# Attention tail of a convolution-and-attention network on one core: final projection by image against final projection by unit

## The chip, the cores and the metric

The kernel runs on one core of a Trainium2 chip. The metric is the device time of one execution in microseconds, the median of three runs.

## What is computed

The input is 8 images of 56x56 positions with 128 channels, all in fp32. A first block (group norm, gated long convolution by FFT, residual) gives `x`. The second block, where the change lies, normalizes `x` by groups, mixes heads within every position and adds the result to `x`:

```python
q, k, v = xs @ Wq.T, xs @ Wk.T, 2 * (xs @ Wv.T)        # 8 heads of 16
q, k, v_h = _l2norm(q), _l2norm(k), _l2norm(v)
attn_head = softmax(einsum('bnhd,bngd->bnhg', v_h, v_h))
q = einsum('bnhg,bngd->bnhd', attn_head, q)
k = einsum('bnhg,bngd->bnhd', attn_head, k)
attn = softmax(einsum('bnhd,bnhe->bnde', k, q))
out = einsum('bnhd,bnde->bnhe', v, attn)
out = transpose(out, (0, 3, 1, 2)).reshape(b, n, HEADS * DIM_HEAD)
out = out @ proj_w.T + proj_b
x = x + out
```

The transpose before the last projection matters here. It runs over (batch, e, position, head) and the result is read again as rows of 128: output row e x 196 + r of an image (e is one of 16 numbers of a head, r one of 196) gathers e of all 8 heads of 16 neighbouring positions. So the output row e x 196 + r needs the attention of positions 16 r to 16 r + 15 alone.

## The kernel before

The program is written by hand: each engine has its list of instructions, and semaphores (`wait_ge`, `then_inc`) order them. Stages follow each other: weights, first normalization and projection, taps, convolution (the longest), its output, and `attend` (from line 989), which starts at about 2214.8 us of the span. Only `attend` and one constant's load are touched.

`attend` cuts the 25088 positions into 56 blocks of 448 (4 tiles of 112), and each block into 2 **units** of 224 positions: 14 groups (`GU`) of 16 positions, with (position, head) on the 128 partitions. There are 112 units (`NU`), 14 per image (`UPI`), and round i of the main loop works at several of them. On PE a round is, in this order:

- `scores(i+1)`: 28 matmuls into `ps_s` (two banks); ScalarE exponentiates (`exp_s`), VectorE masks (`mask`),
- `outputs(i-2)`: 28 matmuls into `ps_o`; VectorE moves them to `oT` (`leave`),
- `mix(i)`: 28 matmuls into `ps_mix`; ScalarE (`leave_mix`) and VectorE (`weigh`) take them, GpSimd spreads k to blocks,
- `logits(i-1)`: 56 matmuls into `ps_l`; ScalarE exponentiates (`exp_l`), VectorE normalizes (`divide`: z_sum, z_inv, p_norm),
- in some rounds a **final group**, `final(b, u)`,
- two `project` calls, the q, k, v projections of tiles 8 rounds ahead, into `ps_qkv` and `ps_qkv_fin` in turn; ScalarE squares and copies them (`copy_in`), VectorE sums and normalizes (`squares`, `clamp`, `normalize`), and ScalarE writes them to memory (`store_heads`), from where SyncE's queue loads them with another layout (`turn`). In every second round ScalarE takes a square root (`root`), for which it loads another table and then the exp table again.

The last projection needs, for a row, one e and the 8 heads of 16 positions, and that is a column of `oT`: 128 (position, head) partitions of group r. The kernel before collects `oT` for a whole image (128 x 16 x 196), and in eight final groups (u = 0 to 7) makes the image's rows: four values of e by 98 of r, each a matmul with `oT`'s 98 columns as the weights and the 128x128 matrix moving, plus a second matmul that adds the residual `x1` through the identity, into the same bank. The bank is `ps_qkv_fin`, the one of the odd projection. VectorE adds the bias, broadcast over partitions (`res`), ScalarE's queue stores. `FINS` sets the rounds: (b + 1) x 14 + 3 + u. So rounds 17 to 24, 31 to 38 and so on have a final group, the six after them none, and the last image's eight groups come behind all units, in rounds 115 to 122. In rounds with a final group, PE waits between its two projections:

```python
if i in FINS:
    b, u = FINS[i]
    pe.wait_ge(f_r, b * 8 + u + 1)
project(bk + 1)
```

Projections end with round 103. The residual `x1` has one buffer, loaded again after an image's last group. In the profile `x_in` of this stage is `x1`, since numbers of buffers are left out of names.

Of the kernel before, what the change touches and what calls it, by code (L numbers as in the profile page):

```python
# [70 lines left out]
def load_weights(nc, t, k):  # L71


    with ExitStack() as ctx:
# [29 lines left out]
                     (k.proj_b[:], t.L1_conv_proj_b.rearrange("(a o) -> a o", a=1).to_broadcast([128, CH]))]  # L104
# [884 lines left out]
def attend(nc, t, k):  # L989
# [12 lines left out]
    RH = RPI // 2  # L1002
    with ExitStack() as ctx:
# [28 lines left out]
        ps_a, ps_m, ps_o, ps_f = (psum(n) for n in ("ps_qkv", "ps_mix", "ps_o", "ps_qkv_fin"))  # L1032
# [4 lines left out]
        x1_loaded = sem("x1_loaded")  # L1037
        out_stored = [sem(f"out_stored{m}") for m in range(4)]
# [5 lines left out]
        o_ps, o_r, f_ps, f_r = (sem(n) for n in ("o_ps", "o_ready", "fin_ps", "fin_ready"))  # L1044
        block = ctx.enter_context(nc.Block())
        FINS = {}
        for b in range(BATCH):
            for u in range(8):
                FINS[(b + 1) * UPI + 3 + u] = (b, u)
        ROUNDS = (BATCH) * UPI + 3 + 8  # L1050
# [46 lines left out]
        def _(pe):  # L1097
# [12 lines left out]
            def scores(i):  # L1110
# [3 lines left out]
                if i:  # L1114
                    pe.wait_ge(s_exp, i)
                v = vb[n % NIN]
# [40 lines left out]
            def final(b, u):  # L1157
                lo, e0 = u // 4 * RH, u % 4 * 4
                if u == 0:
                    pe.wait_ge(o_r, (b + 1) * UPI)  # L1160
                    pe.wait_ge(x1_loaded, 16 * (b + 1))
                if b * 8 + u:
                    pe.wait_ge(f_r, b * 8 + u)
                pe.wait_ge(qkv_read, min(NB * BPB, AHEAD * BPB + 2 * (b * UPI + UPI + 3 + u)))
# [10 lines left out]
            for i in range(ROUNDS):  # L1175
# [9 lines left out]
                if i in FINS:  # L1185
                    final(*FINS[i])
                if bk < NB * BPB:
                    project(bk)
                    if i in FINS:
                        b, u = FINS[i]  # L1190
                        pe.wait_ge(f_r, b * 8 + u + 1)
                    project(bk + 1)

        @block.scalar
        def _(act):
# [43 lines left out]
            def store(b, u):  # L1239
                act.wait_ge(f_r, b * 8 + u + 1)  # L1240
                lo, e0 = u // 4 * RH, u % 4 * 4
                rows = t.out_rows[b * TOK:(b + 1) * TOK].rearrange("(e r) c -> r e c", e=HD)
                act.dma_start(rows[lo:lo + RH, e0:e0 + 4, :], res[u % 4][:]).then_inc(out_stored[u % 4], 16)
                if u == 7 and b + 1 < BATCH:
                    act.dma_start(x1[:], t.X1[b + 1]).then_inc(x1_loaded, 16)

            act.dma_start(x1[:], t.X1[0]).then_inc(x1_loaded, 16)
# [8 lines left out]
            for i in range(ROUNDS + 1):  # L1256
# [9 lines left out]
                if unit(i - 1):  # L1266
                    exp_l(i - 1)
                if bk < NB * BPB:
                    copy_in(bk)
                    copy_in(bk + 1)  # L1270
                if i in FINS:
                    store(*FINS[i])
            for m in range(4):
                act.wait_ge(out_stored[m], 16 * 2 * BATCH)
# [190 lines left out]
```

## Time and profile before

| | |
|---|---|
| median of 3 runs | 3543.01 us (3539.26 to 3554.57) |
| the profiled execution's own time | 3533.34 us |
| its span, first to last instruction | 3531.5 us |
| mean granted TensorE clock | 0.951 |
| PE busy | 3160.9 us, 90% of the span |
| VectorE, ScalarE, GpSimd busy | 2083.4, 1486.9, 251.6 us |
| `attend` in the span | 2214.8 to 3531.5 us |

PE's busy time is made of pipelined matmuls, whose records overlap, and covers time in which it isn't at its peak. What is worth reading is when one group of matmuls starts and the next: the distance of starts, and what PE waited for where there is a gap. A matmul in fp32 has two records (x56 for 28), a transpose one.

### The profile page before, as it was taken

How to read it: one execution, taken by the hardware profiler on the slowest of the kernel's cores; microseconds unless marked ns; L12 is line 12 of the kernel's file. 1: busy time of each engine (PE TensorE's matmuls, PEld its weight loads, DVE VectorE, ACT ScalarE, POOL GpSimd, SP SyncE). 2: the span in 40 equal slices, each digit the busy share in tenths (PEclk: the TensorE clock that was granted, in tenths of full speed). 3: DMA queues.
4: the chain of work that ended last, by engine and by line, in shares of the span. 5: the costliest groups of instructions: out<-in, count | busy, mean ns of one | idle time of the engine just before them, and what ended most of it. 6: DMA issues, size and time to landing. Idle time of an engine off the chain costs nothing. (4 is left out here: it accounts for less than half of the span.)

```text
span 3531.5 us, 106371 instructions
## 1 busy us (share of the span) xinstructions
PE 3160.9 (90%) x44223; PEld 2406.7 (68%) x44223; DVE 2083.4 (59%) x3840; ACT 1486.9 (42%) x3254; POOL 251.6 (7%) x162
## 2 busy tenths in 40 slices
PE   5686977999999999999999898589898989898887
PEld 4563324777777777777777544477777877777777
DVE  4453553666666666666666577455555555555553
ACT  3454422444444444444444344454444444444431
POOL 0000000000000000000000022211111111111111
PEclk8787978999999999999999999799999999999999
DMA  6886004111211211111112497655555555555552
GB/s 149 252 215 177 1 0 160 49 48 48 49 48 48 49 49 48 48 49 49 48 49 49 165 404 311 130 82 87 107 88 106 93 98 88 104 104 87 106 83 52
DMA packets 1033978, 351.36 MB, mean 99 GB/s; under 512 B 888569, under 2 KB 1005991, under 8 KB 1028519
## 3 DMA queue, kind: packets, MB, share of 16 engines
q1 hardware_dynamic: 710832, 198.81, 25.7%
q10 hardware_dynamic: 322807, 147.46, 15.3%
q8 instruction: 282, 4.62, 0.5%
q14 instruction: 57, 0.47, 0.0%
HBM read 174.01 MB, written 172.15 MB: 98 GB/s over the span
## 5 line engine op out<-in xcount | busy, mean ns | idle before, releaser
L751 ACT ACTIVATE x_half<-ps_x 56x228 f32<-56x228 f32 x1024 | 366.1, 357 | 671.8 <-PE ps_x L693 662.9
L801 DVE TENSOR_TENSOR terms<-spec,ps_z 112x456 f32<-112x456 f32 x1024 | 573.0, 621 | 33.8 <-PE ps_z L701 28.7
L708 PEld LDWEIGHTS ps_q<-inv_w,prod 112*114 112x114 f32 x4096 | 434.9, 180 | 27.5 <-issue 25.5
L708 PE MATMUL ps_q<-inv_w,prod 112*114 112x112 f32 x4096 | 451.0, 263 | 0.9 <-DVE prod L805 0.9
L701 PE MATMUL ps_z<-x_half,fwd_w 120*112 120x456 f32 x1024 | 446.4, 558 | 0.9
L811 DVE COPY y_sb<-ps_y 112x224 f32<-112x224 f32 x256 | 100.1, 391 | 414.2 <-PE ps_y L716 331.7
L1143 PE MATMUL ps_l<-q_mixed,k_blocks 32*64 32x64 f32 x12544 | 231.8, 220 | 74.1 <-issue 73.4
L1094 POOL TENSOR_TENSOR k_blocks<-k_mixed,same_of 128x896 f32<-128x896 f32 x112 | 193.8, 1730 | 1072.4 <-ACT k_mixed L1237 1072.4
L1143 PEld LDWEIGHTS ps_l<-q_mixed,k_blocks 32*64 32x64 f32 x12544 | 206.1, 133 | 88.5 <-issue 79.8
L1120 PEld LDWEIGHTS ps_s<-v_blocks 128*64 128x64 f32 x6272 | 200.9, 141 | 90.5 <-issue 79.2
L693 PEld LDWEIGHTS ps_x<-fwd_h,v_in 96*120 96x120 f32 x2048 | 256.2, 185 | 8.0 <-issue 3.2
L693 PE MATMUL ps_x<-fwd_h,v_in 96*120 96x114 f32 x2048 | 256.2, 268 | 1.7 <-ACT x_half L751 1.7
L716 PEld LDWEIGHTS ps_y<-q_half,inv_h 114*112 114x112 f32 x1024 | 179.2, 176 | 114.8 <-issue 95.2
L701 PEld LDWEIGHTS ps_z<-x_half,fwd_w 120*112 120x112 f32 x1024 | 160.7, 176 | 124.9 <-issue 111.6
L1120 PE MATMUL ps_s<-v_blocks 128*64 128x64 f32 x6272 | 218.9, 228 | 23.2 <-issue 14.7
L716 PE MATMUL ps_y<-q_half,inv_h 114*112 114x224 f32 x1024 | 236.4, 352 | 1.3 <-ACT q_half L778 1.3
L1132 PE MATMUL ps_mix<-qk_rows,e_blocks 64*64 64x64 f32 x6272 | 212.9, 220 | 10.0 <-issue 9.8
L1154 PE MATMUL ps_o<-p_norm,v_blocks 128*64 128x64 f32 x6272 | 208.6, 224 | 11.3 <-DVE p_norm L1327 8.0
L1305 DVE TENSOR_TENSOR e_blocks<-s_exp,same_of 128x896 f32<-128x896 f32 x112 | 121.9, 1088 | 153.6 <-ACT s_exp L1222 153.6
L1132 PEld LDWEIGHTS ps_mix<-qk_rows,e_blocks 64*64 64x64 f32 x6272 | 195.1, 135 | 20.2 <-issue 12.3
L1154 PEld LDWEIGHTS ps_o<-p_norm,v_blocks 128*64 128x64 f32 x6272 | 198.0, 140 | 12.6 <-DVE p_norm L1327 8.1
L1281 DVE TENSOR_REDUCE nsq<-sq 112x48 f32<-112x768 f32 x112 | 106.7, 953 | 161.4 <-ACT qkv L1206 161.4
(128 smaller groups left out, 4488.7 us busy)
## 6 DMA issues: line engine op xcount, KB each, us to landing
conv_in<-v_sb ACTq DMA_DIRECT2D x112, 256.0 KB, 3.3
v_in<-conv_in SPq DMA_DIRECT2D x256, 112.0 KB
qk_heads<-st_qk ACTq DMA_DIRECT2D x56, 476.0 KB, 4.7
qk_rows<-qk_heads SPq DMA_DIRECT2D x56, 476.0 KB, 6.7
conv_out<-y_sb ACTq DMA_DIRECT2D x512, 49.0 KB
y<-conv_out SPq DMA_DIRECT2D x8, 1792.0 KB, 13.5
x_in<-in_x SPq DMA_DIRECT2D x8, 1568.0 KB, 9.7
shortcut<-short ACTq DMA_DIRECT2D x8, 1568.0 KB, 6.3
```

The lines of the kernel that those rows point to most:

```text
L693: last = pe.matmul(ps_x[0:120, c * 2 * NF:(c + 1) * 2 * NF], v_in[b % 2][:, c * 2 * PADW:c * 2 * PADW + 120], k.fwd_h[:], start=True, stop ...
L701: last = pe.matmul(ps_z[b % 2][x][0:NFFT, 0:PC], k.fwd_w[:, x, :], x_half[b % 2][:].rearrange("p c a f -> p (c a f)"), start=True, stop=True)
L708: last = pe.matmul(ps_q[0:2 * NF, c * NFFT:(c + 1) * NFFT], prod[b % 2][:, x, c * 2 * NF:(c + 1) * 2 * NF], k.inv_w[:, x, :], start=(x == ...
L716: last = pe.matmul(ps_y[0:2 * SIDE, 0:CC // 2 * SIDE], k.inv_h[:, x, :], q_half[:, :, x, :], start=(x == 0), stop=(x == 1))
L751: last = act.activation(x_half[b % 2][to:to + SIDE, :, a], src, ACT.Copy)
L801: last = dve.tensor_tensor(terms[:, x, :], spec[a][:, s, :], ps_z[b % 2][z][0:NFFT, 0:PC], ALU.mult)
L1094: pool.tensor_tensor(kb[i % 2][:], bcast(km[i % 2][:], 3, 4), bcast(bcast(k.same4[:], 1, HD), 1, GU), ALU.mult).then_inc(k_r, 1)
L1120: last = pe.matmul(to, v[:, gb, a, :], v[:, gb, a, :], start=True, stop=True)
L1132: last = pe.matmul(ps_m[rows, g * QKM:g * QKM + 64], eb[i % 2][rows, g, :], strided(qk[n % NIN][rows], gb * QKW, [[1, 64]]), start=True, s ...
L1143: last = pe.matmul(ps_l[half:half + 64, s // 2, g * HD:g * HD + 64], kb[i % 2][rows, g].rearrange("p d m -> p (d m)"), qm[i % 2][rows, g:g ...
L1154: last = pe.matmul(ps_o[64 * a:64 * a + 64, g * HD:g * HD + 64], vb[n % NIN][:, gb, a, :], pn[i % 2][:, a, g:g + 4, :], start=True, stop=True)
L1305: dve.tensor_tensor(eb[i % 2][:], ex[i % 2][:], bcast(k.same8[:], 1, GU), ALU.mult).then_inc(e_r, 1)
```

## The change

The final projection is made per unit, with the output channels on the partitions:

- `final(i)` is one matmul: the 128x128 matrix as the weights, `oT` of the unit (now 128 x 16 x 14, two buffers) as 224 moving columns, into the first bank of `ps_s`, where the scores of unit i + 3 have just been read. It stands in round i + 2, behind the logits.
- VectorE adds bias (now one number per partition) and residual in one scalar_tensor_tensor (`add`) and writes `y_fin`.
- `turn_out(i)`, in round i + 3, transposes `y_fin` in two halves of 112 columns into `ps_o`; ScalarE copies them (`copy_out`), and its queue stores them in two transfers.
- `x1` has two buffers, and those of the first two images are loaded at the start.
- `FINS` and the eight rounds behind the last unit are gone (`ROUNDS` is `NU + 4`), as is PE's wait between projections. `ps_qkv_even` and `ps_qkv_odd` are new names of the projections' banks.
- New waits: `scores(i)` for `add(i-4)`, `outputs(i)` for `copy_out(i-2)` in place of `leave(i-1)`, `turn_out(i)` for `add(i)` and `leave(i+1)`.

```diff
@@ attend @@
-        oT = [sb(f"oT{m}", [128, HD, RPI]) for m in range(2)]
-        x1 = sb("x1_in", [128, TOK])
-        res = [sb(f"res{m}", [RH, 4, CH]) for m in range(4)]
+        oT, y1 = ([sb(f"{n}{m}", [128, HD, GU]) for m in range(2)] for n in ("oT", "y_fin"))
+        x1 = [sb(f"x1_in{m}", [128, HD, RPI]) for m in range(2)]
+        res = [sb(f"res{m}", [TB, 2, CH]) for m in range(3)]
...
-        ROUNDS = (BATCH) * UPI + 3 + 8
+        ROUNDS = NU + 4
@@ PE: scores @@
                 if i:
                     pe.wait_ge(s_exp, i)
+                if i >= 4:
+                    pe.wait_ge(f_r, i - 3)
@@ PE: outputs @@
                 pe.wait_ge(p_r, i + 1)
-                if i:
-                    pe.wait_ge(o_r, i)
+                if i >= 2:
+                    pe.wait_ge(t_r, i - 1)
@@ PE @@
-            def final(b, u):
-                lo, e0 = u // 4 * RH, u % 4 * 4
...
-                for e in range(4):
-                    to = ps_f[0:RH, e * CH:(e + 1) * CH]
-                    pe.matmul(to, oT[b % 2][:, e0 + e, lo:lo + RH], k.w[:, PW, :], start=True, stop=False)
-                    at = (e0 + e) * RPI + lo
-                    last = pe.matmul(to, x1[:, at:at + RH], k.ident[:], start=False, stop=True)
-                last.then_inc(f_ps, 1)
+            def turn_out(i):
+                pe.wait_ge(f_r, i + 1)
+                pe.wait_ge(o_r, min(i + 2, NU))
+                if i:
+                    pe.wait_ge(t_r, i)
+                for h in range(2):
+                    last = pe.transpose(ps_o[0:TB, h * CH:(h + 1) * CH], y1[i % 2][:, 8 * h:8 * h + 8, :].rearrange("p e g -> p (e g)"), k.ident[:])
+                last.then_inc(t_ps, 1)
+
+            def final(i):
+                pe.wait_ge(o_r, i + 1)
+                pe.wait_ge(s_exp, min(i + 4, NU))
+                pe.matmul(ps_s[:, 0, 0:HD * GU], k.w[:, PW, :], oT[i % 2][:].rearrange("p e g -> p (e g)"), start=True, stop=True).then_inc(f_ps, 1)
@@ PE: the round, behind logits(i - 1) @@
-                if i in FINS:
-                    final(*FINS[i])
+                if unit(i - 3):
+                    turn_out(i - 3)
+                if unit(i - 2):
+                    final(i - 2)
                 if bk < NB * BPB:
                     project(bk)
-                    if i in FINS:
-                        b, u = FINS[i]
-                        pe.wait_ge(f_r, b * 8 + u + 1)
                     project(bk + 1)
@@ ScalarE @@
+            def copy_out(i):
+                m = i % 3
+                act.wait_ge(t_ps, i + 1)
...
+                act.activation(res[m][:].rearrange("p h c -> p (h c)"), ps_o[0:TB, 0:2 * CH], ACT.Copy).then_inc(t_r, 1)
+
+            def store(i):
+                m, b, r0 = i % 3, i // UPI, i % UPI * GU
+                act.wait_ge(t_r, i + 1)
+                rows = t.out_rows[b * TOK:(b + 1) * TOK].rearrange("(h e r) c -> h e r c", h=2, e=8)
+                for h in range(2):
+                    act.dma_start(rows[h, :, r0:r0 + GU, :], res[m][:, h, :]).then_inc(out_stored[m], 16)
...
@@ VectorE @@
             def leave(i):
...
+            def add(i):
                 b, r0 = i // UPI, i % UPI * GU
+                dve.wait_ge(f_ps, i + 1)
...
+                if i >= 2:
+                    dve.wait_ge(t_ps, i - 1)
+                dve.scalar_tensor_tensor(out=y1[i % 2][:], in0=ps_s[:, 0, 0:HD * GU].rearrange("p (e g) -> p e g", g=GU), scalar=k.proj_b[:, 0:1],
+                                         in1=x1[b % 2][:, :, r0:r0 + GU], op0=ALU.add, op1=ALU.add).then_inc(f_r, 1)
@@ VectorE: the round, behind divide(i - 1) @@
-                if i in FINS:
-                    add_bias(*FINS[i])
+                if unit(i - 2):
+                    add(i - 2)
```

How the order moves on PE. Before, a round with a final group, from its logits to the next round's outputs (`x27` counts matmuls of one form):

```order
L1143 MATMUL ps_l<-q_mixed,k_blocks 64x64 [waits l_exp_ready,k_blocks_ready,q_mixed_ready]
L1143 MATMUL ps_l<-q_mixed,k_blocks 64x64 x55
L1167 MATMUL ps_qkv_fin<-weights,oT 98x128 [waits qkv_read,fin_ready]
L1169 MATMUL ps_qkv_fin<-ident,x_in 98x128
...
L1104 MATMUL ps_qkv<-weights,xn_in 112x384 [waits qkv_read,xn_loaded0]
L1104 MATMUL ps_qkv_fin<-weights,xn_in 112x384 [waits qkv_read,fin_ready]
L1120 MATMUL ps_s<-v_blocks 64x64 [waits s_exp_ready,in_loaded2]
L1120 MATMUL ps_s<-v_blocks 64x64 x27
L1154 MATMUL ps_o<-p_norm,v_blocks 64x64 [waits o_ready,p_ready]
```

Changed, the same place, in every round:

```order
L1140 MATMUL ps_l<-q_mixed,k_blocks 64x64 [waits l_exp_ready,k_blocks_ready,q_mixed_ready]
L1140 MATMUL ps_l<-q_mixed,k_blocks 64x64 x55
L1160 MATMUL ps_o<-ident,y_fin 112x128 [waits turned_ready,o_ready,fin_ready]
L1160 MATMUL ps_o<-ident,y_fin 112x128
L1166 MATMUL ps_s<-oT,weights 128x224 [waits s_exp_ready,o_ready]
L1099 MATMUL ps_qkv_even<-weights,xn_in 112x384 [waits qkv_read]
L1099 MATMUL ps_qkv_odd<-weights,xn_in 112x384 [waits qkv_read]
L1117 MATMUL ps_s<-v_blocks 64x64 [waits fin_ready,s_exp_ready]
L1117 MATMUL ps_s<-v_blocks 64x64 x27
L1151 MATMUL ps_o<-p_norm,v_blocks 64x64 [waits turned_ready,p_ready]
```

The wait for `fin_ready` has moved from the odd projection in some rounds to the scores in all of them. On VectorE, changed, where it is set:

```order
L1331 TENSOR_REDUCE z_sum<-p_exp 128x28 [waits l_exp_ready]
L1333 RECIPROCAL z_inv<-z_sum 128x28 [waits z_ready]
L1337 TENSOR_TENSOR p_norm<-p_exp,z_inv 128x2x224 [waits o_ps,z_inv_ready]
L1354 SCALAR_TENSOR_TENSOR y_fin<-ps_s,proj_b,x_in 128x224 [waits turned_ps,fin_ps]
L1291 TENSOR_REDUCE nsq<-sq 112x48 [waits qkv_read]
```

`y_fin`, which sets `fin_ready`, stands where `res` (98x512, line 1343) stood in rounds with a final group, now in every round.

## Rows read from the trace of the kernel before

**Rows 1.** Windows: busy us of each engine (x instructions), PEclk, DMA share, GB/s.
```profile
2275.60:3468.20 1192.60, 1062.55 (x31266) 912.20 (x31265) 664.27 (x1221) 546.69 (x1201) 185.41 (x107) 0.98 0.55 94
...
2589.00:2683.00 94.00, 85.77 (x2407) 73.72 (x2408) 53.19 (x98) 42.59 (x95) 13.68 (x8) 1.00 0.56 93
```

**Rows 2.** Timeline, PE, scores opening rounds 2, 17, 25, 31, 39, 109.
```profile
2275.60 0.62 PE L1120 MATMUL ps_s<-v_blocks 128*64 128x64 f32 x13
...
2432.21 0.50 PE L1120 MATMUL ps_s<-v_blocks 128*64 128x64 f32 x9
...
2527.08 0.51 PE L1120 MATMUL ps_s<-v_blocks 128*64 128x64 f32 x10
...
2588.97 0.51 PE L1120 MATMUL ps_s<-v_blocks 128*64 128x64 f32 x10
...
2682.82 0.50 PE L1120 MATMUL ps_s<-v_blocks 128*64 128x64 f32 x9
...
3468.20 0.62 PE L1120 MATMUL ps_s<-v_blocks 128*64 128x64 f32 x13
```

**Rows 3.** Timeline, PE, round 72, without a final group.
```profile
3053.49 1.85 PE L1120 MATMUL ps_s<-v_blocks 128*64 128x64 f32 x56
...
3060.47 0.90 PE L1104 MATMUL ps_qkv<-weights,xn_in 128*112 128x384 f32 x2
...
3061.94 0.28 PE L1120 MATMUL ps_s<-v_blocks 128*64 128x64 f32 x2
```

**Rows 4.** Timeline, PE, round 77, with one.
```profile
3122.01 0.46 PE L1167 MATMUL ps_qkv_fin<-weights,oT 128*98 128x128 f32 x2
...
3125.02 0.90 PE L1104 MATMUL ps_qkv_fin<-weights,xn_in 128*112 128x384 f32 x2 [0.37 <-DVE res L1343]
3125.84 0.34 PE L1120 MATMUL ps_s<-v_blocks 128*64 128x64 f32 x4
```

**Rows 5.** Waits of PE, rounds 2 to 109: total us, times, longest us.
```profile
PE ps_l L1143 <- issue: 73.4, 57, 3.1
```

**Rows 6.** Timeline, PE, transposes of the first stage.
```profile
252.48 0.55 PE L285 MATMUL ps_turn<-ident,x_in 112*128 112x112 f32 x4
252.86 0.86 PE L290 MATMUL ps_sumsq<-ones,x_sq 128*112 128x1 f32 x8
```

**Rows 7.** Timeline, VectorE, round 77.
```profile
3122.72 0.62 DVE L1321 TENSOR_REDUCE z_sum<-p_exp 128x28 f32<-128x448 f32 x1 [1.08 <-ACT p_exp L1228]
...
3123.74 0.62 DVE L1327 TENSOR_TENSOR p_norm<-p_exp,z_inv 128x448 f32<-128x448 f32 x1
3124.28 0.68 DVE L1343 TENSOR_TENSOR res<-ps_qkv_fin,proj_b 98x512 f32<-98x512 f32 x1
```

**Rows 8.** Timeline, ScalarE, then VectorE, round 72.
```profile
3054.81 1.28 ACT L1210 ACT_TABLE_LOAD   x1
...
3060.31 0.39 DVE L1316 TENSOR_TENSOR q_mixed<-ps_mix,d_sq_inv 128x224 f32<-128x224 f32 x1
3061.18 0.62 DVE L1321 TENSOR_REDUCE z_sum<-p_exp 128x28 f32<-128x448 f32 x1 [0.48 <-ACT p_exp L1228]
```

**Rows 9.** Groups, VectorE: busy us, mean ns | idle before, releaser.
```profile
L1335 DVE TENSOR_TENSOR oT<-ps_o,qk_rows 128x224 f32<-128x224 f32 x112 | 62.3, 556 | 10.3 <-PE ps_o L1154 10.3
...
L1316 DVE TENSOR_TENSOR q_mixed<-ps_mix,d_sq_inv 128x224 f32<-128x224 f32 x112 | 43.8, 391 | 5.3 <-DVE d_sq_inv L1311 0.2
...
L383 DVE SCALAR_TENSOR_TENSOR short<-xT,biases,xg 128x448 f32<-128x448 f32 x56 | 37.6, 672 | 0.5
```

**Rows 10.** Timeline, PE and the ACT queue, at the end.
```profile
3506.57 0.46 PE L1167 MATMUL ps_qkv_fin<-weights,oT 128*98 128x128 f32 x2 [0.65 <-DVE oT L1335]
...
3528.73 0.33 ACTq L1243 DMA_DIRECT2D out<-res  x1
```

**Rows 11.** Groups, ScalarE; then DMA issues (KB, us to landing).
```profile
L1204 ACT ACTIVATE sq<-ps_qkv 112x256 f32<-112x256 f32 x112 | 43.0, 384 | 161.9 <-PE ps_qkv L1104 155.2 <-issue 3.3 <-DVE st_v L1298 3.3
...
x_in<-x_mid ACTq DMA_DIRECT2D x8, 1568.0 KB, 7.9
```

More of the change, by code:

```diff
@@ L1028, in attend @@
         pn = [sb(f"p_norm{m}", [128, 2, GU + 3, HD]) for m in range(2)]
-        oT = [sb(f"oT{m}", [128, HD, RPI]) for m in range(2)]
-        x1 = sb("x1_in", [128, TOK])
-        res = [sb(f"res{m}", [RH, 4, CH]) for m in range(4)]
-        ps_a, ps_m, ps_o, ps_f = (psum(n) for n in ("ps_qkv", "ps_mix", "ps_o", "ps_qkv_fin"))
+        oT, y1 = ([sb(f"{n}{m}", [128, HD, GU]) for m in range(2)] for n in ("oT", "y_fin"))
+        x1 = [sb(f"x1_in{m}", [128, HD, RPI]) for m in range(2)]
+        res = [sb(f"res{m}", [TB, 2, CH]) for m in range(3)]
+        ps_a, ps_m, ps_o, ps_f = (psum(n) for n in ("ps_qkv_even", "ps_mix", "ps_o", "ps_qkv_odd"))
         ps_s, ps_l = psum("ps_s", (128, 2, 512)), psum("ps_l", (128, 2, 512))
@@ L1036, in attend @@
         in_loaded = [sem(f"in_loaded{m}") for m in range(NIN)]
-        x1_loaded = sem("x1_loaded")
-        out_stored = [sem(f"out_stored{m}") for m in range(4)]
+        x1_loaded = [sem(f"x1_loaded{m}") for m in range(2)]
+        out_stored = [sem(f"out_stored{m}") for m in range(3)]
         cleared, k_r, qkv_ps, qkv_read = sem("cleared"), sem("k_blocks_ready"), sem("qkv_ps"), sem("qkv_read")
@@ L1043, in attend @@
         l_ps, l_exp, z_r, zi_r, p_r = (sem(n) for n in ("l_ps", "l_exp_ready", "z_ready", "z_inv_ready", "p_ready"))
-        o_ps, o_r, f_ps, f_r = (sem(n) for n in ("o_ps", "o_ready", "fin_ps", "fin_ready"))
+        o_ps, o_r, f_ps, f_r, t_ps, t_r = (sem(n) for n in ("o_ps", "o_ready", "fin_ps", "fin_ready", "turned_ps", "turned_ready"))
         block = ctx.enter_context(nc.Block())
[L1046 to L1049, printed above, removed]
-        ROUNDS = (BATCH) * UPI + 3 + 8
+        ROUNDS = NU + 4
         def unit(i):
@@ L1237, in leave_mix, with load_x1 @@
                 act.activation(km[i % 2][:], ps[:, :, HD + 1:], ACT.Copy).then_inc(km_r, 1)
[L1239 to L1247, printed above, removed]
+            def load_x1(b):
+                act.dma_start(x1[b % 2][:].rearrange("p e r -> p (e r)"), t.X1[b]).then_inc(x1_loaded[b % 2], 16)
+            def copy_out(i):
+                m = i % 3
+                act.wait_ge(t_ps, i + 1)
+                if i >= 3:
+                    act.wait_ge(out_stored[m], 32 * (i // 3))
+                act.activation(res[m][:].rearrange("p h c -> p (h c)"), ps_o[0:TB, 0:2 * CH], ACT.Copy).then_inc(t_r, 1)
[5 more added lines that the diff above has]
+                    act.dma_start(rows[h, :, r0:r0 + GU, :], res[m][:, h, :]).then_inc(out_stored[m], 16)
+                if i % UPI == UPI - 1 and b + 2 < BATCH:
+                    act.wait_ge(f_r, (b + 1) * UPI)
+                    load_x1(b + 2)
+            for b in range(2):
+                load_x1(b)
             for bk in range(AHEAD * BPB):
@@ L1267, in _ @@
                     exp_l(i - 1)
+                if unit(i - 3):
+                    copy_out(i - 3)
                 if bk < NB * BPB:
@@ L1270, in _ @@
                     copy_in(bk + 1)
-                if i in FINS:
-                    store(*FINS[i])
-            for m in range(4):
-                act.wait_ge(out_stored[m], 16 * 2 * BATCH)
+                if unit(i - 3):
+                    store(i - 3)
+            for m in range(3):
+                act.wait_ge(out_stored[m], 32 * ((NU - 1 - m) // 3 + 1))
         @block.vector
@@ L1387, in build @@
         k.rpe_in = sb("rpe_in", [3, 128])
-        k.proj_b = sb("proj_b", [128, CH])
+        k.proj_b = sb("proj_b", [128, 1])
         k.same4, k.same8 = sb("same_of_4", [128, 4]), sb("same_of_8", [128, 64])
```

30 lines of the change are left out of this document (9 added, 21 removed).

## The prediction

> **What bounds the kernel now.** I read the page first (the diff touches the last stage alone), then the timeline of that stage by engine, then its waits. Scores of one round to scores of the next make a round. Between the scores of round 2 and those of round 109 lie 1192.60 us, 107 rounds of 11.15 us, in which PE is busy 1062.55 us at a mean clock of 0.98 [rows 1, 2]. So PE is what ends a round; the other engines follow it. Of the 107 rounds, 56 carry a final group (8 for each of seven images, rounds 17 to 24, 31 to 38 and so on) and 51 do not.
>
> A round without a disturbance shows the clean price. Scores at 3053.49, the first projection at 3060.47, the next scores at 3061.94: 6.98 us from scores to the end of the logits, and a **gap** of 1.47 us for the two projections, 8.45 us in all [rows 3]. With a final group the gap is 3122.01 to 3125.84, 3.83 us: the finals, the projections, and 0.37 us in which the second of these waits for VectorE's `res` [rows 4]. Such a round is 6.98 + 3.83 = 10.81 us clean.
>
> Real rounds are longer. Two groups of 8 final rounds, 2432.21 to 2527.08 and 2588.97 to 2682.82, take 188.72 us, 11.80 each; the 6 rounds between them take 61.89 us, 10.32 each [rows 2]. The **rest** over clean is 0.99 us with a final group and 1.87 us without. Most of it is PE idle with "issue" as releaser, 73.4 us ahead of the logits alone, in 57 stalls [rows 5]. The same instructions stall less where the gap is longer.
>
> **What the change takes away.** The eight matmuls of a final group, their wait, the wait of the odd projection for `res`, and the burst after the last unit. With it goes VectorE's `res` (0.68 us, 64 times).
>
> **What it puts into each round's gap, on PE.** Two transposes: four of 112 columns follow each other in 252.86 - 252.48 = 0.38 us, 0.10 each [rows 6]; at 128 columns 0.11 each, 0.22. One projection with 224 moving columns: the ones with 384 columns stand 0.74 us apart (half of 1.47), so 0.43. PE alone would need 0.22 + 0.43 + 1.47 = 2.12 us for the gap.
>
> **What it puts behind the logits, on VectorE.** `scores(i+2)` now waits for `f_r`, which is `add(i-2)`, since the final projection borrows `ps_s`. In VectorE's order `add` stands behind `divide`, and `divide` needs the logits just ended. From the end of the logits (3122.01) z_sum starts 0.71 us later, p_norm at 3123.74, and the next VectorE operation at 3124.28, 2.27 us after the logits [rows 7]. That chain has the same length in a round without a final group (z_sum at 3061.18, 0.71 after 3060.47 [rows 3, 8]). Then comes `add`, an operation the trace does not have in this shape. From below: a tensor_tensor from PSUM on 128x224 takes 0.391 us. From above: `res` with 512 elements, 0.68. A scalar_tensor_tensor on 448 elements takes 0.672 against 0.62 of p_norm, a tensor_tensor on as many, so the second operation with its scalar costs 0.05 [rows 7, 9]. I take 0.391 + 0.05 = 0.44, nearest to the operation with the same 224 elements, and 0.05 us to PE, as from `res` to the projection behind it (3124.28 + 0.68 = 3124.96, 3125.02) [rows 4, 7]. The gap is 2.27 + 0.44 + 0.05 = **2.76 us**, 0.64 more than PE needs: a new wait of PE ahead of the scores in every round. Clean round: 6.98 + 2.76 = 9.74.
>
> **The rest over clean.** Bounds 0.99 and 1.87. The new gap is 1.29 us longer than the short one, of the 2.36 between short and long, which in proportion gives 1.39; a disturbance of up to 0.64 us that falls in the gap disappears in the wait, so I take 1.30. A round is 11.04, 107 of them 1181.3, against 1192.6: **-11.3 us**.
> The Trainium skill (Runtime: NRT & Kernel Launch, section Instruction fetch mechanics) has instructions refilled in 16 KiB blocks at a cost it calls mostly hidden. Here it isn't hidden, if the "issue" stalls are these refills. By that rule the rest would be 0 on both sides: now 51 x 8.45 + 56 x 10.81, less 5 x 1.84 for the last five final rounds, which have no projections, 1027; changed 107 x 9.74 = 1042; +15 in place of -11.
>
> **The end.** Now the first final matmul of the last eight groups starts at 3506.57, the last store is issued at 3528.73 and the span ends at 3531.5, 2.8 later [rows 10]. Changed: one projection of 224 columns from 3506.57 until about 3507.2 (0.43 and the pipe's latency), `add` 0.44 to 3507.7, two transposes to 3508.1, one copy of 112x256 at 0.384 [rows 11] to 3508.6, then the same 2.8 for the store: 3511.5, **-20**. Round 109 and what follows it has a longer gap, +1.
>
> **The beginning.** Two images of the residual are loaded at once instead of one; one takes 7.9 us to land [rows 11] and it lies ahead of the first stores of heads on the same queue, which come some 20 us after. Between 0 and 8, I take +2.
>
> **Costed at nothing.** The bias column load, one of many loads; `leave` writing a smaller tile. ACT's copy (0.384) follows the logits' exp while PE still transposes and projects, and outputs two steps on need it only 1.7 us into the next round. Two stores per unit are issued at 0.33 each [rows 10] on ACT's queue, ahead of the square root's table load of every other round, behind which stand s_exp, the mask, `leave`, and so `turn_out` and z_sum. Now that load starts at 3054.81, 1.32 us after the scores, and VectorE ends q_mixed at 3060.70, 0.48 before z_sum [rows 8]. With the change ACT's copies of qkv end 0.65 later, the scores start 1.29 later, and the stores add 0.66: 0.02 later against the scores. If the cover of 0.48 goes, each us more costs a us in every other round.
>
> Sum: -11.3 - 20 + 1 + 2 = **-28 us**. The profiled execution took 3533.34 us (span 3531.5); it becomes 3505. It stands 9.7 below the median of 3543.0, so a median of **3515** is predicted.
>
> **The rivals.**
> 1. *The stalls shrink as far as in rounds with a final group.* Even spread helps every refill. Rest 0.99: 107 x 10.73 = 1148.1, -44.5, with the ends -61.5: 3482. For it: the whole drop came with a gap that held PE for 2.36 us longer, and the first part of it may do most. Against: only 0.64 is pure waiting.
> 2. *`add` is as dear as `res`,* by strided reading or PSUM access: 0.68 gives a gap of 3.00, +26: 3541. For it: `oT`, which also has strided operands, takes 0.556 with 224 elements [rows 9].
> 3. *The other side: the stalls stay as in rounds without a final group.* They sit mostly ahead of the logits [rows 5], and that stretch has its 6.98 us of the same instructions whatever the gap. Rest 1.87: 107 x 11.61 = 1242.3, +49.7, with the ends +33: 3576. It turns the sum positive from a rest of 1.56, and past 0.5% from 1.73. Against it: final rounds, with the same instructions there, have 0.99.
> 4. *The clock falls.* With idle time in every gap the granted clock could drop more often than its 0.98 [rows 1]. At 0.94, a half-clock share of 12% in place of 4%, 8% of 9.1 us of work in 107 rounds adds 78: 3593. The final groups, which wait 0.37 in each round, ran at 1.00 between 2589 and 2683, which speaks against it [rows 1]. The Trainium skill (TensorE: Matmul & The Clock Gate, A second HAM failure mode: psum-queue depth-cycling) describes this swing for a kernel that idles briefly between groups.
> 5. *The burst at the end isn't shortened,* since the chain through five engines is slower than counted: 3535.
>
> **How the numbers follow.** Forecast 0.45, rival 1 0.18, rival 2 0.20, rival 3 0.11, rival 4 0.04, rival 5 0.02. A measurement of this kernel can tell about 0.5% (17.7 us) from no change: faster means below 3525.3. Of the forecast 0.37 lies there and 0.08 within; with rival 1 faster is 0.55; rivals 2 and 5 and that 0.08 make 0.30 the same; 3 and 4 make 0.15 slower. The range, 3480 to 3565, reaches to half of rivals 1 and 3 and leaves out 0.19.
>
> **What would show it.** PE idle ahead of `ps_s` with `y_fin` as releaser, 0.6 us in nearly each of 104 rounds or more; a gap of 2.7 to 2.8 in clean rounds; `y_fin` at 0.44; "issue" idle ahead of the logits of 50 to 70 us between the scores of rounds 2 and 109, now 73.4 [rows 5]; the last scores to the end 20 shorter. I am wrong if PE does not wait for `y_fin` (the chain was not last), if 6.98 has grown (outputs or `turn_out` waiting), or if the clock is under 0.96.

## The result, and the profile after

| | before | changed |
|---|---|---|
| median, range | 3543.91 us (3539.26 to 3554.57, 4 runs) | 3590.56 us (3584.89 to 3596.18, 4 runs) |
| profiled execution, span | 3533.34, 3531.5 us | 3586.99, 3585.1 us |
| scores of round 2 to scores of round 109 | 1192.60 us | 1251.57 us |

The changed kernel takes 1.0128 times as long (95% interval 1.0112 to 1.0144). 3515 was predicted, with 3565 as the upper end; it is slower by more than the 0.5% that can be told from no change.

Windows of the changed kernel, columns as in [rows 1]:

```profile
2290.74:3542.31 1251.57, 1035.63 (x30796) 893.31 (x30795) 672.79 (x1271) 571.81 (x1305) 181.90 (x107) 0.96 0.53 90
```

PE is busy 27 us less than before and the stretch is 59.0 us longer, at a mean clock of 0.96 after 0.98 [rows 1]. The profiled executions differ by 53.7 us. These 59.0 are the main part. The tail behind the scores of round 109 is 42.8 us after 63.3, -20.5; from `attend`'s start to round 2 it is 63.4 after 60.8, +2.6; the stages ahead of `attend`, which the change doesn't touch, end 12.5 us later. That last part is scatter: a second profile of the kernel before, below, reaches round 2 at 2289.17, the first at 2275.60 [rows 2].

A round without a disturbance, changed kernel, timeline of PE and then of VectorE; it answers to [rows 3, 4, 7]:

```profile
3072.01 1.85 PE L1117 MATMUL ps_s<-v_blocks 128*64 128x64 f32 x56 [0.74 <-DVE y_fin L1354]
...
3078.99 0.43 PE L1160 MATMUL ps_o<-ident,y_fin 128*112 128x128 f32 x2
3079.26 0.54 PE L1166 MATMUL ps_s<-oT,weights 128*128 128x224 f32 x2
3079.64 0.81 PE L1099 MATMUL ps_qkv_even<-weights,xn_in 128*112 128x384 f32 x2
3080.29 0.81 PE L1099 MATMUL ps_qkv_odd<-weights,xn_in 128*112 128x384 f32 x2
3081.86 0.36 PE L1117 MATMUL ps_s<-v_blocks 128*64 128x64 f32 x5 [0.76 <-DVE y_fin L1354]
```

```profile
3079.71 0.62 DVE L1331 TENSOR_REDUCE z_sum<-p_exp 128x28 f32<-128x448 f32 x1 [1.48 <-ACT p_exp L1223]
...
3080.72 0.62 DVE L1337 TENSOR_TENSOR p_norm<-p_exp,z_inv 128x448 f32<-128x448 f32 x1
3081.27 0.44 DVE L1354 SCALAR_TENSOR_TENSOR y_fin<-ps_s,proj_b,x_in 128x224 f32<-128x224 f32 x1
```

From the scores to the end of the logits it is 6.98 us, as before. The new wait of PE for `y_fin` is there, and the gap is 3081.86 - 3078.99 = 2.87 us. The clean round is 9.85.

Waits of PE between the scores of rounds 2 and 109: total us, times, longest us. The releaser "issue" means that PE waited for nothing that the profile shows. The first row answers to [rows 5], which has 73.4.

```profile
PE ps_l L1140 <- issue: 96.4, 61, 4.3
PE ps_s L1117 <- DVE y_fin L1354: 67.5, 84, 2.1
PE ps_o L1151 <- issue: 24.9, 17, 2.5
PE ps_mix L1129 <- issue: 11.5, 19, 1.3
```

The "issue" stalls grew by 23 us ahead of the logits, and by 22 us ahead of the outputs, for which the same view of the kernel before has:

```profile
PE ps_o L1154 <- issue: 3.2, 5, 1.0
```

A mean round is 1251.57 / 107 = 11.70 us. Its rest over clean is 1.85, where I had taken 1.30. Of these 198 us in 107 rounds, 145 are "issue" stalls of over 0.3 us, and at most 46 are lost to the lower clock (both below).

**Where the stalls lie.** Timeline of PE, changed kernel, from one stall to the fifth:

```profile
2673.14 0.32 PE L1160 MATMUL ps_o<-ident,y_fin 128*112 128x128 f32 x1 [1.11 <-issue]
2673.30 0.58 PE L1166 MATMUL ps_s<-oT,weights 128*128 128x224 f32 x2
2673.72 0.81 PE L1099 MATMUL ps_qkv_even<-weights,xn_in 128*112 128x384 f32 x2
2674.36 0.81 PE L1099 MATMUL ps_qkv_odd<-weights,xn_in 128*112 128x384 f32 x2
2675.10 1.85 PE L1117 MATMUL ps_s<-v_blocks 128*64 128x64 f32 x56
2676.78 1.80 PE L1151 MATMUL ps_o<-p_norm,v_blocks 128*64 128x64 f32 x56
2678.52 0.44 PE L1129 MATMUL ps_mix<-qk_rows,e_blocks 64*64 64x64 f32 x6
2680.15 1.67 PE L1129 MATMUL ps_mix<-qk_rows,e_blocks 64*64 64x64 f32 x50 [1.20 <-issue]
2681.75 1.39 PE L1140 MATMUL ps_l<-q_mixed,k_blocks 32*64 32x64 f32 x78
2684.45 0.79 PE L1140 MATMUL ps_l<-q_mixed,k_blocks 32*64 32x64 f32 x34 [1.31 <-issue]
2685.17 0.43 PE L1160 MATMUL ps_o<-ident,y_fin 128*112 128x128 f32 x2
2685.44 0.55 PE L1166 MATMUL ps_s<-oT,weights 128*128 128x224 f32 x2
2685.82 0.81 PE L1099 MATMUL ps_qkv_even<-weights,xn_in 128*112 128x384 f32 x2
2686.46 0.81 PE L1099 MATMUL ps_qkv_odd<-weights,xn_in 128*112 128x384 f32 x2
2688.00 1.85 PE L1117 MATMUL ps_s<-v_blocks 128*64 128x64 f32 x56 [0.73 <-DVE y_fin L1354]
2689.66 1.02 PE L1151 MATMUL ps_o<-p_norm,v_blocks 128*64 128x64 f32 x28
2692.36 1.03 PE L1151 MATMUL ps_o<-p_norm,v_blocks 128*64 128x64 f32 x28 [1.69 <-issue]
2693.33 1.85 PE L1129 MATMUL ps_mix<-qk_rows,e_blocks 64*64 64x64 f32 x56
2695.11 0.91 PE L1140 MATMUL ps_l<-q_mixed,k_blocks 32*64 32x64 f32 x43
2697.49 0.69 PE L1140 MATMUL ps_l<-q_mixed,k_blocks 32*64 32x64 f32 x32 [1.47 <-issue]
```

Add the counts from stall to stall: 125, 128, 126 and 127 matmul records. Each has its weight load, and a few separate semaphore instructions stand between them: 256 instructions each time. Counting all of PE's records from the scores of round 2 on, all stalls of over 0.3 us, 95 in the kernel before and 96 in the changed one, end at one position modulo 256, give or take one. No other modulus from 200 to 599 gathers more than 49 of them, and that one is 512. From here on 256 instructions of PE are a **block** (not the 448 positions of `attend`). Block ends come in any part of a round, since a round has some 583 instructions, 2.3 blocks (before 572, with a final group 607).

The view of the transfers names what comes once per block, between the scores of rounds 2 and 109 (packets, MB, share of 16 engines):

```profile
q8 instruction: 243, 3.98, 1.3%
```

243 packets of 16 KB for 243 blocks (before: 247). In the timeline above they landed at 2671.74, 2678.68, 2682.90, 2691.00 and 2695.97, and PE went on 1.40, 1.47, 1.55, 1.36 and 1.52 us later. Over all 64 stalls of over 1 us the median is 1.44. So a stall is the wait for a refill of instructions. One starts about 2 us after a block's end (median 1.96), takes 0.97 (median; mean 1.08), and is usable 1.44 later: typically 4.4 us from one block's end until the next may end freely. The starts scatter: a tenth of them come within some 0.5 us, and a tenth later than 3.8 us before and 5.3 us changed. So 4.4 us is no sharp bound.

Now the two kernels by how long a block runs:

| block runs | before: blocks, stall in all, mean | changed |
|---|---|---|
| under 3.2 us (mean 2.6; nearly nine in ten end in the logits) | 55, 66.4 us, 1.21 | 55, 90.8 us, 1.65 |
| 3.2 to 5 us | 135, 43.1 us, 0.32 | 101, 26.4 us, 0.26 |
| 5 us and more (they hold a gap) | 55, 0.0 us, 0 | 86, 28.1 us, 0.33 |

The logits are 224 instructions in 1.8 us; scores, outputs and mix 112 each in 1.7. A block that ends in the logits runs for 2.6 us and mostly stalls. The gap lies behind them, in the next block, which had time to spare already. Lengthening the gap gives time to the blocks that need none.

That tells why the stalls did not shrink. They grew as well, by 36 us, and what goes with that is when the refill starts. Those of the short blocks start on average 1.8 us after the previous block's end before (1.6 in experiment 11's profile), 2.5 changed (2.4 in experiment 8's). Experiments 1 and 12 have 2.2 and 2.5, and 7 has 1.5; the short blocks' mean stalls below go up and down with it. What moves the starts is not shown.

### The profile page after: what moved, and what is told of

Its sections match the earlier page's. It is cut to its first block and busy times, and to the rows that moved or that the text cites. A ratio compares the mean times of both kernels' runs of the same rounds, so it can differ in the third digit from the quotient of the medians.

```text
span 3585.1 us, 105957 instructions
## 1 busy us (share of the span) xinstructions
PE 3134.7 (87%) x43647; PEld 2378.5 (66%) x43647; DVE 2087.6 (58%) x3888; ACT 1514.7 (42%) x3366; POOL 248.6 (7%) x162
## 5 line engine op out<-in xcount | busy, mean ns | idle before, releaser
L1331 DVE TENSOR_REDUCE z_sum<-p_exp 128x28 f32<-128x448 f32 x112 | 69.4, 620 | 262.3 <-ACT p_exp L1223 262.3
L1129 PEld LDWEIGHTS ps_mix<-qk_rows,e_blocks 64*64 64x64 f32 x6272 | 201.1, 138 | 23.2 <-issue 14.8
```

The lines of the kernel that those rows point to most:

```text
L1129: last = pe.matmul(ps_m[rows, g * QKM:g * QKM + 64], eb[i % 2][rows, g, :], strided(qk[n % NIN][rows], gb * QKW, [[1, 64]]), start=True, s ...
L1331: dve.tensor_reduce(zs[a][:], pe_[a][:], AX, ALU.add).then_inc(z_r, 1)
```

## The experiments

All are compared with the kernel before on the same chip. "Stalls" are those of over 0.3 us at the ends of blocks, summed between the scores of rounds 2 and 109. Where a diff is only a part of an edit, "..." marks what is left out. The texts of the first four were written before I had counted instructions, and argue only from the length of the gap and what PE does in it.

**1. Swap the two borrowed banks.** The final projection goes to `ps_o`, the transposes to `ps_s`, so the scores no longer need this round's `y_fin`.

```diff
-                if i >= 4:
-                    pe.wait_ge(f_r, i - 3)
+                if i >= 5:
+                    pe.wait_ge(t_r, i - 4)
...
-                    last = pe.transpose(ps_o[0:TB, h * CH:(h + 1) * CH], ...
+                    last = pe.transpose(ps_s[0:TB, 0, h * CH:(h + 1) * CH], ...
...
-                pe.matmul(ps_s[:, 0, 0:HD * GU], k.w[:, PW, :], ...
+                pe.matmul(ps_o[:, 0:HD * GU], k.w[:, PW, :], ...
...
```

> The changed kernel with two banks exchanged: the final projection goes to ps_o and the transposes to ps_s, so that the scores wait for ScalarE's copy (some 1.1 us behind the logits) and no more for y_fin. PE's own work in the gap is 2.12 us, so a clean round should be 9.1 to 9.2 us in place of 9.85. Theory A (PE's rest of 1.85 us per round comes of stalls for instructions that a queue full of long matmuls would hide, and that a wait does not hide): the rest stays at 1.7 to 2.0, 107 rounds become 70 to 80 us shorter, about 3512. Rival B (the wait ahead of the scores brings the stalls itself, since PE's sequencer cannot run ahead): the rest falls below 1.5 too, 110 us or more shorter, 3480. Rival C (longer time alone hides stalls, as the prediction had it): the rest grows by 0.3, 40 us shorter only, 3550.

Measured: 3507.09 us, ratio 0.9914 (0.9890 to 0.9939). Clean round 9.01, gap 2.03, rest 1.93, stalls 134.8 us, the short blocks at 1.49 each. The gap, PE:

```profile
2982.48 0.43 PE L1160 MATMUL ps_s<-ident,y_fin 128*112 128x128 f32 x2
...
2984.51 1.85 PE L1117 MATMUL ps_s<-v_blocks 128*64 128x64 f32 x56
```

The same final projection per unit, without PE's wait, is faster than the kernel before. So the wait is what makes the change slow, and it bought nothing: the rest is as high without it. But 25 of the 36 us by which the stalls grew are here too, without the wait. That part comes with something else of the change, which no run singles out.

**2. Fill the wait with work.** The odd projection is computed twice.

```diff
+                if bk % 2 and bk >= AHEAD * BPB:
+                    pe.matmul(ps_f[0:TB, 0:3 * CH], ..., start=True, stop=True)
```

> The changed kernel, with the odd projection of each round computed twice into its bank, which fills 0.65 us of the 0.75 us wait ahead of the scores with work that needs few instructions. A clean round stays 9.85. Theory A (a full queue hides stalls): the rest per round falls from 1.85 towards 1.3, 50 us shorter than the changed kernel, 3540. Rivals B and C (the wait brings the stalls; only time counts): B gives a fall as well, if the wait shrinks to 0.1; C gives no difference, 3590.

Measured: 3586.64 us, ratio 1.0128 (1.0067 to 1.0188), the changed kernel's. PE's wait for `y_fin` falls from 67.5 to 8.9 us. Clean round 9.84, rest 1.85, stalls 133.5. Whether PE works or waits in the gap makes no difference to the rest.

**3. Put a wait of this kind into the kernel before,** ahead of the scores.

```diff
+                if i >= 3:
+                    pe.wait_ge(p_r, i - 2)
```

> The kernel before, with scores(i) waiting for divide(i - 3). In rounds without a final group PE then waits about 1.0 us ahead of the scores (p_norm ends 2.35 us behind the logits, the gap is 1.47), in rounds with one not at all. 51 rounds, clean price +1.0 each. Theory A (waiting hides nothing): the rest of these rounds stays at 1.87, +51 us, 3595. Rival C (time alone hides stalls, the step of the prediction): their rest falls by 0.4, +30 us, 3573. Rival B (a wait brings stalls): the rest rises above 2.2, +70 us or more, 3615.

Measured: 3609.62 us, ratio 1.0213 (1.0166 to 1.0260). Ordinary clean rounds 9.48 after 8.45; their rest stays, 1.95 (before 1.98 as a mean over all 51). Stalls 127.8 after 109.5. A longer gap in the kernel before takes nothing off the rest either. The time was forecast at 3595, and what is over comes from the rounds with a final group: they have no new wait, their clean round stays 10.82, and they take 12.20 us on average after 11.79, 23 us in all. So the wait also costs something in the rounds beside it.

**4. Leave out the stores of the result** (all but the last unit's, so the output is not written).

```diff
+                if i >= NU - 1:
                     for h in range(2):
                         act.dma_start(rows[h, :, r0:r0 + GU, :], ...
```

> The changed kernel without its 222 output stores (two for the last unit remain); the output is left unwritten. Tests whether two stores per unit, 0.68 us each on ScalarE's queue and 57 KB each of DMA, cost PE anything: by delaying ScalarE or by making instruction refills slower. Theories A, B and C: within 5 us of the changed kernel, 3588. Rival D (the transfers slow the refills): the rest falls by 0.3 or more, 35 us shorter, 3555.

Measured: 3573.05 us, ratio 1.0116 (1.0068 to 1.0163). Clean round 9.84, rest 1.71, stalls 127.2. The stretch is 16 us shorter than in the changed kernel, so 222 transfers beside the refills cost that at most, and a refill takes 1.04 us on average after 1.08; the medians, from different comparisons, don't separate the two.

**5. Spread the slow instructions** (on experiment 1): the two projections stand in the middle of the logits. From here on the reading above, by which a block that runs too short waits for its refill, is theory R.

```diff
                 for g in range(GU):
+                    if g in (5, 10) and bk < NB * BPB:
+                        project(bk + g // 5 - 1)
                     for s in range(4):
...
```

> Theory R (refills): TensorE's queue reads its instructions in blocks of 256 (16 KB). In the traces of both kernels and of the first four experiments every stall of the queue sits at one and the same position of 256: in the kernel before 95 stalls, 110 us, all at a block's end. A refill starts about 2 us after a block's end, takes 1.07 us, and the queue goes on 1.44 us after it landed, some 4.4 us in all; a block that runs for less than 3.2 us (those that end in the logits, 2.6 us) therefore stalls for 1.2 to 1.7 us, and one that holds the gap (5 us and more) hardly ever. Here the banks are swapped as in the first experiment (3507 us; stalls 136 us, of it 86 us at 58 short blocks), and the two projections stand in the middle of the logits, so that 224 instructions there take 3.1 us rather than 1.8. Theory R expects next to no block under 3.2 us, stalls of 75 us rather than 136, and with fewer half-clock windows 3430 us (3400 to 3470), with clean rounds of 9.0 to 9.2 us as there. Rival T (the refills are limited by their total number, or by the transfers beside them): the number of instructions is the same, so stalls stay at 136 us and the time at 3507.

Measured: 3503.27 us, ratio 0.9895 (0.9871 to 0.9919). Stalls 50.6 us after 134.8, 3 short blocks after 58, clock 0.99. The instructions and the refills are as many as before: theory R holds and T falls. The time was missed (3430 forecast), since the clean round went from 9.01 to 10.18. The timeline shows where:

```profile
2994.43 0.81 PE L1142 MATMUL ps_l<-q_mixed,k_blocks 32*64 32x64 f32 x40
...
2995.18 0.90 PE L1099 MATMUL ps_qkv_even<-weights,xn_in 128*112 128x384 f32 x2
...
2996.00 0.67 PEld L1142 LDWEIGHTS ps_l<-q_mixed,k_blocks 32*64 32x64 f32 x40 [0.56 <-issue]
```

Behind a projection, the weight load of the next small matmuls starts 0.56 us after the loads before it have ended. That is not peculiar to the 32-row tiles of the logits; experiment 1 has the same ahead of the scores, once a round:

```profile
2984.51 1.71 PEld L1117 LDWEIGHTS ps_s<-v_blocks 128*64 128x64 f32 x56 [0.56 <-issue]
```

Here it comes twice within the logits. From 2994.43 to the transposes at 2998.20 it is 3.77 us, where clean logits take 1.79 and the two projections 1.38 (0.64 + 0.74) in experiment 1: +0.60. Another 0.28 of the 1.17 is a wait of the scores for ScalarE's copy of the turned result, 29.6 us in 104 rounds, which the projections had covered. The last 0.3 is not traced to one place.

**6. The same in the kernel before,** with the even projection alone.

```diff
                 for g in range(GU):
+                    if g == 7 and bk < NB * BPB:
+                        project(bk)
...
```

> The kernel before with one of the round's two projections moved from the gap into the middle of the logits, nothing else. Theory R: the short blocks run 0.65 us longer and those in the gap, which have time to spare, as much shorter; stalls fall from 110 to 70-80 us, time 3535 to 3490-3510. Rival T: no change, 3535.

Measured: 3558.97 us, ratio 1.0050 (1.0022 to 1.0078). Stalls 69.6 us after 109.5, as theory R has it. The time is missed again by a wait: with one projection fewer ahead of it, the odd projection waits 50.7 us for `res` rather than 14.8, and the clean rounds are 8.79 (8.45) and 11.80 (10.82).

**7. The control: the same projections between scores and outputs** (on experiment 1).

```diff
                     scores(i + 1)
+                if bk < NB * BPB:
+                    project(bk)
+                    project(bk + 1)
                 if unit(i - 2):
                     outputs(i - 2)
...
```

> The same move as in the spread kernel, of the same two projections out of the gap, but to a place between scores and outputs, where the blocks already run 4 us and more. Theory R: the blocks that end in the logits stay at 2.6 us, stalls stay at 125 to 145 us, time 3507 within 15. If moving the projections out of the gap helps for any other reason (their banks come free sooner, ScalarE's copies start elsewhere), this kernel shows it as well as the spread one does.

Measured: 3523.00 us, ratio 0.9946 (0.9923 to 0.9970). The 60 short blocks stay and run 2.68 us, as R has it, and the move gives no gain in time. But the stalls fell to 97.3, under the 125 expected: a short block stalls 1.16 here, 1.49 in experiment 1. So its own length is not all that counts; how early its refill starts does too (1.5 us after the previous block's end on average, 2.2 in experiment 1), and I can't forecast that from the order of the instructions. The clean round rose from 9.01 to 9.70 meanwhile, in part by a wait of the scores for ScalarE's copy, 26.2 us in 95 rounds. So the time shows only the sum of the two, and the control is clean in the short blocks' number and length alone.

**8. The changed kernel once more.**

> The changed kernel once more, unchanged, for a second profile: how far do stalls and clean rounds differ from one execution to the next? Theory R: clean round 9.85 us, stalls 130 to 150 us, all at a block's end. Time 3590 (3575 to 3600). If the stalls came down to the 110 us of the kernel before, their growth in the first profile was chance.

Measured: 3585.00 us; stretch 1252.04, clean round 9.84, stalls 144.1 us (145.3 in the first profile). The growth is no chance.

**9. Transposes and one projection straight ahead of the logits** (on experiment 1), and ScalarE's copy ahead of the logits' exp.

```diff
+                if unit(i - 3):
+                    turn_out(i - 3)
+                if bk < NB * BPB:
+                    project(bk)
                 if unit(i - 1):
                     logits(i - 1)
-                if unit(i - 3):
-                    turn_out(i - 3)
                 if unit(i - 2):
                     final(i - 2)
                 if bk < NB * BPB:
-                    project(bk)
                     project(bk + 1)
...
```

> Banks swapped as in the first experiment; the two transposes and one of the projections stand straight ahead of the logits, the other projection stays behind the final one; the copy of the turned result is made ahead of the logits' exp. A block that ends in the logits has at most 224 instructions of them, so it holds the slow ones straight ahead of them too: 0.27 us of transposes and 0.65 of a projection. Theory R: short blocks of 2.65 us become 3.5, stalls fall from 136 us to 75-90; the clean round, 9.01 there, pays one change from a full-height matmul to the logits' 32-row tiles (in the spread kernel 0.6 us of the 1.17 that its clean round was longer by, for two such changes): 9.0 to 9.3. Time 3440 to 3485, 3460 likeliest. Rival T (number of refills decides): 3507 or more.

Measured: **3469.93 us**, ratio 0.9791 (0.9763 to 0.9819), the fastest. Windows, and a clean round:

```profile
2288.98:3425.33 1136.35, 1028.36 (x30795) 868.46 (x30794) 657.72 (x1268) 563.03 (x1305) 194.14 (x107) 0.99 0.58 99
```

```profile
2969.00 0.43 PE L1160 MATMUL ps_s<-ident,y_fin 128*112 128x128 f32 x2
2969.27 0.81 PE L1099 MATMUL ps_qkv_even<-weights,xn_in 128*112 128x384 f32 x2
2970.01 1.86 PE L1140 MATMUL ps_l<-q_mixed,k_blocks 32*64 32x64 f32 x112
2971.80 0.65 PE L1165 MATMUL ps_o<-oT,weights 128*128 128x224 f32 x2
2972.28 0.81 PE L1099 MATMUL ps_qkv_odd<-weights,xn_in 128*112 128x384 f32 x2
2973.02 1.85 PE L1117 MATMUL ps_s<-v_blocks 128*64 128x64 f32 x56
```

Ahead of the logits the projection costs little (clean round 9.21 after 9.01), and every block that ends in them now holds it. 14 short blocks are left, stalls 98.5 us, time at 1.2 GHz 27 us after 75. The time is where it was put, the stalls are over the 75 to 90 expected: most of them, 78 us, now stand at blocks of 3.2 to 5 us. So the bound of 3.2 us in the table marks where stalls get shorter, not where they end.

**10. Both projections ahead of the logits.**

> As the one before, with both projections ahead of the logits. Theory R: short blocks become 4.2 us, stalls 55-75 us; but only the final projection and the scores are left between logits and outputs, some 2.2 us, where p_norm is ready 2.36 us after the logits' end in the spread kernel's trace: outputs wait for it, clean round 9.2 to 9.5. Time 3440 to 3500.

Measured: 3478.56 us, ratio 0.9824 (0.9797 to 0.9851). Stalls 79.1 us, but the clean round is 9.79: outputs wait 29.0 us for `y_fin`, which shares their bank. I had expected a wait for p_norm, which is 0.5 us, and a clean round of 9.2 to 9.5.

**11. The kernel before once more.**

> The kernel before once more, unchanged: how far do its stalls differ from one execution to the next? Theory R: 105 to 120 us, with ordinary rounds over 1.2 us and final rounds under 0.9 each; time 3540. If the final rounds came out at 1.0 or more, the low rest of the final rounds in the first profile, on which the prediction took its value, was chance.

Measured: 3539.69 us; stalls 101.9 us (109.5 in the first profile), final rounds 0.71 (0.75) and the others 1.22 (1.33). So final rounds do stall less; that was no chance.

**12. Put the wait back into experiment 1.**

```diff
+                if i >= 4:
+                    pe.wait_ge(f_r, i - 3)
```

> The first experiment's kernel (banks swapped, no wait of TensorE for y_fin, 3507 us) with that wait put back ahead of the scores, though its banks don't need it. Theory W: the wait alone is what the changed kernel loses: clean round 9.8, 3575 to 3600 us, and, as no refill starts in the wait, stalls of 140 to 150 us rather than 136, the growth at blocks of 5 us and more. Rival B (the sharing of banks costs beside the wait): clean round 9.85 but time at most 3560.

Measured: 3596.40 us, ratio 1.0153 (1.0123 to 1.0184); clean round 9.84, stalls 145.7 us, with the growth where it was expected: blocks of 5 us and more hold 24 us of stalls, 9 in experiment 1. Windows, and the waits:

```profile
2286.81:3547.38 1260.57, 1042.15 (x30796) 895.84 (x30795) 672.49 (x1272) 572.25 (x1305) 181.71 (x107) 0.96 0.53 90
```

```profile
PE ps_l L1142 <- issue: 101.9, 64, 4.3
PE ps_s L1119 <- DVE y_fin L1355: 67.5, 82, 2.1
```

The one wait takes the ratio from 0.9914 to 1.0153, which is all that the changed kernel loses against experiment 1. Sharing the banks costs nothing beside it.

The rest is a mean round less a clean one. In the first row the last five rounds with a final group, which have no projections, are allowed for; doing the same for experiment 5 would make its 0.73 some 0.8.

| kernel | stretch | clean round | rest | short blocks, mean stall | stalls | at 1.2 GHz |
|---|---|---|---|---|---|---|
| before (11) | 1192.6 (1188.3) | 8.45 / 10.82 | 1.55 (1.51) | 55, 1.21 (55, 1.13) | 109.5 (101.9) | 41 (44) |
| changed (8) | 1251.6 (1252.0) | 9.85 | 1.85 (1.86) | 55, 1.65 (57, 1.52) | 145.3 (144.1) | 92 (85) |
| 1 swap | 1171.1 | 9.01 | 1.93 | 58, 1.49 | 134.8 | 75 |
| 12 swap, wait | 1260.6 | 9.84 | 1.94 | 55, 1.66 | 145.7 | 99 |
| 5 spread | 1167.0 | 10.18 | 0.73 | 3, 1.34 | 50.6 | 21 |
| 9 one ahead | 1136.4 | 9.21 | 1.41 | 14, 1.55 | 98.5 | 27 |

## Why the prediction was wrong, point by point

**The step that failed** is "I take 1.30" for the rest over clean, from "in proportion" and "a disturbance of up to 0.64 us that falls in the gap disappears in the wait". The rest is 1.85: 107 x 0.55 = 58.9 us of the 70.3 by which -11.3 and +59.0 differ. I read 1.87 without and 0.99 with a final group (1.98 and 1.14 over all rounds, not only the 22 of the rows) as a function of the gap's length, since that was what differed in the rows. But the gap changes the blocks that hold it, and those had stalled for 0.0 us in 55 blocks already. Most of the stall time is in the blocks that end in the logits, as [rows 5] said, and rival 3 had the sentence for it: that stretch has the same instructions whatever the gap. It was given 0.11, and came true to the size: rest 1.87 there, 1.85 here; 3576 there, 3590.6 here. The size is in part luck: rival 3 has the stalls unchanged, and they grew from 109.5 to 145.3 us. Its 1.87 was read from rounds without a final group; over all rounds before, the rest was 1.55.

Why final rounds have the lower rest is shown in part. They stalled 0.71 and 0.75 us a round in two profiles, mostly since blocks of 3.2 to 5 us stall 0.17 there and 0.44 in the others (experiment 11 has 0.15 and 0.44), and short ones 1.04 instead of 1.41. A final group adds eight matmuls (16 records), which lengthen the blocks they fall in and put block ends elsewhere. Which of the two does it was not tried, and it isn't robust: with the wait of experiment 3 the same rounds stall 1.01.

**The gap** of 2.76 is 2.87: 107 x 0.11 = 11.8 us, the other part of the 70.3. The chain to the end of p_norm is 2.28 (forecast 2.27) and `y_fin` 0.44, as said; from its end at 3081.71 to the scores it is 0.15, where I had taken 0.05 from `res` to a projection.

**The wait** on `y_fin` is where it was put and has its size: 67.5 us in 84 rounds. That it is the loss is shown by experiments 1 and 12. What it does beyond its length is only argued, and it is small: 11 us of stalls between experiments 1 and 12. Of some 243 refills, 31 to 34 start in the last us of a round in the kernel before and in experiment 1, 2 to 5 in the five profiles where PE stands at a wait there (the changed kernel twice, 3, 4 and 12). A reading is that a queue that stands doesn't ask for its next block, so the refill comes later. It fits that blocks of 5 us and more stall 0.24 to 0.35 in those and not at all before. But experiment 1, without a wait, has 0.21, and experiment 2, where the wait is filled and 10 refills start there, has 0.29. So this stays open.

**The clock** was rival 4's. It fell from 0.98 to 0.96, with 23 stretches at 1.2 GHz of together 92 us, after 11 of 41 us. In 22 of the 23 PE stood at an "issue" stall of 1.7 us or more when the clock fell, or up to 1.6 us before; in the last, at a wait of 2.0 for `y_fin`. Half speed can lose at most half of it, 46 us after 20, and that is within the rest. It comes with the stalls and goes with them (experiments 5 and 9). The price of 78 us for a clock of 0.94 was too high: 9.1 us of work at a mean of 0.94 in place of 0.98 take 0.39 longer, 41 us in 107 rounds.
The Trainium skill (TensorE: Matmul & The Clock Gate, A second HAM failure mode: psum-queue depth-cycling) speaks of idling between groups; experiment 2, where a further projection leaves 8.9 us of the wait for `y_fin`, still has 68 us at 1.2 GHz with its 133.5 us of stalls, and experiment 1, with no such wait, has 75. So the short idle in each gap isn't needed for it here.

**Refills taken as hidden,** which the prediction weighed, would have left only the clean rounds, +15 us. The clean rounds came to 107 x 9.85 = 1054, +27, which is that and the 12 of the gap; the rest was not hidden.
The Trainium skill (Runtime: NRT & Kernel Launch, Instruction fetch mechanics) states blocks of 256 instructions in 16 KiB, and this trace agrees, with stalls at 256 and 243 packets of 16 KB; that crossing a block is mostly hidden doesn't hold here, with 145 us of stalls in 1252.

**Right:** 6.98 us to the end of the logits unchanged; `add` at 0.44, so rival 2 falls; the end 20.5 shorter (20 forecast, less 1 for round 109), so rival 5 falls; the beginning +2.6 (+2). A store is issued in 0.68 us, not 0.33, with no loss seen in the clean round.

## What to carry to other kernels

When PE stalls on "issue", count the instructions between two stalls before giving them a cause. If they come every 256, a block must run longer than about 4.4 us here to be free in the typical case, and what helps is slow instructions inside the dense stretch, not a pause behind it: moving one projection and two transposes from behind the logits to ahead of them took the ratio from 0.9914 to 0.9791 with nothing added. A borrowed bank is cheap only where its reader is done early: the same projection in the other of two banks was worth 2.1% of the time (1.0128 against 0.9914). And a mean that differs between two kinds of rounds isn't a slope: ask which part of the round carries it.

## What was not expected of the hardware

- The landed block is not usable at once: PE goes on 1.44 us (median of 64) after the refill's record ends, in every kernel within 0.1.
- Refills took 1.03 to 1.08 us each on average, yet over ten in a row they never started closer than 4.29 us apart on average in the kernel before, the changed one and experiments 1, 5, 9 and 10. In the fastest kernel they came every 4.68 us (1136.35 / 243). With 2.27 blocks to a round and 4.3 to 4.4 us for each, I estimate that this order of work can't go much below 9.8 to 10 us a round, whatever PE's clean round is; fewer instructions would be the next step. That wasn't tried.
- Behind a projection the weight load of the next small matmuls stays idle for 0.56 us, ahead of the scores (experiment 1) as in the logits (experiment 5). Two projections within the logits cost 0.60 there; with one ahead of them the clean round was 0.2 longer.
